# Inverting the chunk matrices of a gated delta rule: 64x64 blocks in two tiles, or 32x32 blocks in four

## The reference

```python
def step(S, inp):
    q_t, k_t, v_t, g_t, b_t = inp
    S = S * jnp.exp(g_t)[..., None, None]
    kv = jnp.einsum('bhk,bhkv->bhv', k_t, S)
    delta = (v_t - kv) * b_t[..., None]
    S = S + k_t[..., :, None] * delta[..., None, :]
    o = jnp.einsum('bhk,bhkv->bhv', q_t, S)
    return (S, o)
```

## Time and profile before

| | us |
|---|---|
| median of 3 runs | 808.12 (807.68 to 809.06) |
| the profiled execution | 807.6 |
| its span, first to last instruction | 805.9 |
| TensorE busy in the span | 662.2 (82%) |
| VectorE busy | 404.2 (50%) |
| ScalarE busy | 324.5 (40%) |

### The profile page before, as it was taken

One profiled execution on the slowest core, in us unless ns is written; L12 is line 12 of the kernel. 1 busy time (PEld: TensorE's weight loads), 2 busy tenths in 40 slices (PEclk: granted clock), 3 DMA queues, 4 the chain that ended last, 5 costly groups with the idle time before them and its releaser, 6 DMA issues. The chain is left out here.

```text
span 805.9 us, 19964 instructions
## 1 busy us (share of the span) xinstructions
PE 662.2 (82%) x8150; PEld 506.7 (63%) x8150; DVE 404.2 (50%) x911; ACT 324.5 (40%) x881; POOL 136.9 (17%) x211
## 2 busy tenths in 40 slices
PE   5789989898999999957875999989895652479995
PEld 3456666655666666635664466689895541479885
DVE  6437788854355555145773557457646463011111
ACT  1245555525444444425773541521243230233331
POOL 2012110120000000033333420650000213111121
PEclk9779999999999999958887889999998775699999
DMA  6930000036000000040000000000000038881110
GB/s 173 352 102 2 3 2 2 16 122 142 1 2 1 2 1 2 1 133 2 2 2 2 0 2 2 1 2 0 2 1 1 0 102 296 315 297 51 43 48 23
DMA packets 33165, 45.36 MB, mean 56 GB/s; under 512 B 7998, under 2 KB 26175, under 8 KB 32960
## 3 DMA queue, kind: packets, MB, share of 16 engines
q1 hardware_dynamic: 28672, 33.31, 12.7%
q0 software_dynamic: 2256, 7.37, 2.8%
q10 hardware_dynamic: 2160, 3.60, 1.5%
HBM read 36.91 MB, written 7.89 MB: 56 GB/s over the span
## 5 line engine op out<-in xcount | busy, mean ns | idle before, releaser
L387 ACT ACTIVATE a_pr<-a_bank,a_nms 128x160 f32<-128x160 f32 x128 | 49.1, 391 | 41.4 <-DVE a_nms L723 38.2
L2118 ACT ACTIVATE f_hb<-f_bank,cols 128x128 f32<-128x128 f32 x96 | 34.9, 367 | 63.2 <-PE f_bank L2236 58.5
L2236 PE MATMUL f_bank<-f_xts,f_w 128*128 x384 | 51.1, 291 | 0.8 <-DVE f_xts L2188 0.8
L2236 PEld LDWEIGHTS f_bank<-f_xts,f_w 128*128 128x128 f32 x384 | 49.9, 207 | 1.7 <-issue 1.2
L2246 PE MATMUL f_bank<-f_w,f_hb 128*128 128x256 f32 x192 | 43.7, 381 | 0.0
L627 DVE TENSOR_REDUCE a_negmx<-a_bank 128x2 f32<-128x320 f32 x64 | 30.5, 476 | 23.0 <-PE a_bank L859 23.0
L2246 PEld LDWEIGHTS f_bank<-f_w,f_hb 128*128 128x128 f32 x192 | 35.9, 192 | 4.4
L2197 DVE TENSOR_TENSOR f_yb<-f_bank,rows 128x256 f32<-128x256 f32 x12 | 5.1, 425 | 58.1 <-PE f_bank L2246 58.1
L358 POOL TENSOR_TENSOR a_spr<-a_linv,a_hm 128x128 f32<-128x128 f32 x32 | 12.1, 398 | 124.3 <-DVE a_linv L676 111.5
L624 DVE COPY a_pt<-a_bank 128x512 f32<-128x512 f32 (+1 forms) x48 | 28.6, 595 | 8.3 <-PE a_bank L868 5.7
L1843 PE MATMUL e_ps<-e_ht,e_wqkv 128*128 128x512 f32 x64 | 31.5, 646 | 1.4 <-DVE e_cv L1728 1.4
(11 more groups left out here) (368 smaller groups left out, 1575.8 us busy)
## 6 DMA issues: line engine op xcount, KB each, us to landing
f_w<-in_f_w SPq DMA_DIRECT2D x16, 1024.0 KB, 10.0
slots<-a_zero POOLq DMA_DIRECT2D x1, 4112.0 KB, 18.1
f_xs<-slots ACTq DMA_DIRECT2D x13, 257.0 KB, 2.7
a_ct<-in_ctxt SPq DMA_DIRECT2D x15, 160.0 KB, 6.1
rows<-in_rows SPq DMA_DIRECT2D x1, 2120.0 KB, 9.4
x<-in_x SPq DMA_DIRECT2D x2, 512.0 KB, 5.0
b_wq<-in_b_wq SPq DMA_DIRECT2D x1, 1024.0 KB, 7.8
b_wk<-in_b_wk SPq DMA_DIRECT2D x1, 1024.0 KB, 9.8
```

What stands on the lines that cost most here:

```text
L387: i = act.activation(pr[:, p, j, k, :], s_bank[j][:, k * KW:(k + 1) * KW], ACT.Exp, bias=nms[:, p, j, k:k + 1], accum_out=rsum[:, p, 2 * j ...
L2118: act.activation(hb[:, m, :], bank[m % 4][:, 0:P], ACT.Gelu, bias=c.col("f_b1", e * FC + m)).then_inc(z["act"], 1)
L2236: j = pe.matmul(bank[m % 4][:, 0:P], w1[:, e, kk, m * P:(m + 1) * P], xts[:, bass.ds(i % 2, 1), kk, :].rearrange("p b n -> p (b n)"), star ...
```

## The change

The inverse is built on the 32x32 diagonal blocks of each system, and the 64x64 level apart:

- `x_`, `xT`, `y` and `lm` are now 32 columns a block, with four 32x32 blocks below one another in the partitions: both halves of both systems. ScalarE copies the diagonal blocks of `lT` into a tile `lc` (`diagonal`, eight copies of 32x512, four behind silu(5) and four behind silu(6)).
- Level 0 has no product: `xT` is the identity (a sixth row of the mask table) minus the mask's result, and `x_` is its transpose by VectorE's 32x32 block transposes.
- Levels 1 to 4 have y products and `xT` by `y` only; `xT` is made from `x_` by block transposes (`turned`). TensorE's levels are a loop, VectorE's and ScalarE's are written out. A product is 32x32 by 32x32, in one of four tiles on the diagonal.
- The last level works on the one off-diagonal 32x32 block of each system: 64 y products from `lT`, 64 from `y` and `xT`. VectorE writes the negated results into `xbd`, ScalarE copies `xT` onto its diagonal (eight copies of 32x512).
- POOL's two copies of the identity are gone.

```diff
+            def diagonal(r):
+                act.wait_ge(z["lT"], r + 1)
+                for q in range(4):
+                    rows, cols = slice(32 * q, 32 * q + 32), slice(32 * (q % 2), 32 * (q % 2) + 32)
+                    a = act.activation(lc[rows, 16 * r:16 * r + 16, :], lT[rows, 16 * r:16 * r + 16, cols], ACT.Copy)
+                a.then_inc(z["lc"], 1)
...
             act.wait_ge(z["ssq"], 1)
             inverse_lengths(0, bank[0][:, 0:32].rearrange("p (t h) -> p t h", h=HG))
-            with act.Fori(1, LEVELS) as lv:
+            for lv in range(1, LEVELS):
                 for g in range(4):
-                    act.wait_ge(z["y"], 4 * lv + g + 1)
-                    act.activation(y[:, 8 * g:8 * g + 8, :].rearrange("p a n -> p (a n)"), bank[g], ACT.Copy).then_inc(z["yout"], 1)
+                    act.wait_ge(z["y"], 4 * (lv - 1) + g + 1)
+                    act.activation(octet(y, g), bank[g][:, 0:256], ACT.Copy).then_inc(z["yout"], 1)
+            act.wait_ge(z["bdz"], 4)
+            act.wait_ge(z["xt"], 4 * (LEVELS - 1))
+            for r in range(2):
+                for q in range(4):
+                    rows = slice(32 * q, 32 * q + 32)
+                    act.activation(xbd[r][rows, :, rows], xT[rows, 16 * r:16 * r + 16, :], ACT.Copy).then_inc(z["xbd"], 1)
...
+            for g in range(4):
+                dve.transpose(octet(x_, g), octet(xT, g)).then_inc(z["x"], 1)
+            for lv in range(1, LEVELS - 1):
+                if lv < LEVELS - 2:
+                    dve.wait_ge(z["y"], 4 * lv)
+                    mask_level(lv + 1)
                 for g in range(4):
-                    dve.wait_ge(z["zx"], 8 * lv + 2 * g - 7)
-                    dve.tensor_tensor(octet(x_, g), octet(x_, g), bank[4 + g], ALU.subtract).then_inc(z["xt"], 1)
-                    dve.wait_ge(z["zx"], 8 * lv + 2 * g - 6)
-                    dve.tensor_tensor(octet(xT, g), octet(xT, g), bank[g], ALU.subtract).then_inc(z["xt"], 1)
...
+                    dve.wait_ge(z["zx"], 4 * (lv - 1) + g + 1)
+                    dve.tensor_tensor(octet(x_, g), octet(x_, g), bank[4 + g][:, 0:256], ALU.subtract).then_inc(z["x"], 1)
+                    if g:
+                        turned(g - 1, 4 * lv + g)
+                turned(3, 4 * lv + 4)
+            dve.wait_ge(z["bdz"], 4)
+            for r in range(2):
+                dve.wait_ge(z["zx"], 4 * (LEVELS - 2) + 2 * r + 2)
                 for b2 in range(2):
...
             def product(dst, lhs, rhs, g):
 
                 for a in range(8 * g, 8 * g + 8):
-                    for b2 in range(2):
-                        r = slice(64 * b2, 64 * b2 + 64)
-                        i = pe.matmul(dst[r, (a % 8) * S:(a % 8 + 1) * S], lhs[r, a, :], rhs[r, a, :], start=True,
-                                      stop=True, tile_position=(64 * b2, 64 * b2))
+                    for q in range(4):
+                        rows = slice(32 * q, 32 * q + 32)
+                        i = pe.matmul(dst[rows, (a % 8) * 32:(a % 8 + 1) * 32], lhs[rows, a, :], rhs[rows, a, :], start=True,
+                                      stop=True, tile_position=(32 * q, 32 * q))
                 return i
...
+            with pe.Fori(1, LEVELS - 1) as lv:
                 pe.wait_ge(z["lm"], lv + 1)
                 for g in range(4):
-                    pe.wait_ge(z["xt"], 8 * lv - 6 + 2 * g)
+                    pe.wait_ge(z["x"], 4 * lv + g - 3)
                     pe.nop(nofuse=True)
                     product(bank[g], lm, x_, g).then_inc(z["y"], 1)
                 for g in range(4):
                     pe.wait_ge(z["yout"], 4 * lv + g - 3)
+                    pe.wait_ge(z["xt"], 4 * lv + g - 3)
                     pe.nop(nofuse=True)
-                    if not last:
-                        product(bank[4 + g], xT, y, g).then_inc(z["zx"], 1)
-                    product(bank[g], y, xT, g).then_inc(z["zx"], 1)
...
+            pe.wait_ge(z["xbd"], 12)
```

More of the change, by code:

```diff
@@ L1678, in _ @@
             silu(5)
+            diagonal(0)
             tap(7)
             silu(6)
+            diagonal(1)
             silu(7)
@@ L1753, in _, with turned @@
             conv(7)
[L1754 to L1755 removed]
             def mask_level(lv):
[L1758 removed]
+                dve.tensor_tensor(lm[:, :, :], lc[:, :, :], mt[:, lv:lv + 1, :].to_broadcast([P, NB, 32]),
                                   ALU.mult).then_inc(z["lm"], 1)
[L1760 removed]
+            def turned(g, n):
+                dve.wait_ge(z["x"], n)
+                dve.transpose(octet(xT, g), octet(x_, g)).then_inc(z["xt"], 1)
@@ L1770, in _ @@
+            dve.wait_ge(z["xt"], 4)
             mask_level(1)
[L1771 to L1778 removed]
@@ L1947, in level @@
                     pe.wait_ge(z["yout"], 4 * lv + g - 3)
+                    pe.wait_ge(z["xt"], 4 * lv + g - 3)
                     pe.nop(nofuse=True)
-                    if not last:
-                        product(bank[4 + g], xT, y, g).then_inc(z["zx"], 1)
-                    product(bank[g], y, xT, g).then_inc(z["zx"], 1)
-            with pe.Fori(1, LEVELS - 1) as lv:
-                level(lv, False)
-            level(LEVELS - 1, True)
-            pe.wait_ge(z["xt"], 8 * (LEVELS - 1) + 4)
+                    product(bank[4 + g], xT, y, g).then_inc(z["zx"], 1)
+            for g in range(4):
+                pe.wait_ge(z["x"], 4 * (LEVELS - 2) + g + 1)
+                for a in range(8 * g, 8 * g + 8):
+                    for b2 in range(2):
+                        low, high = slice(64 * b2, 64 * b2 + 32), slice(64 * b2 + 32, 64 * b2 + 64)
+                        i = pe.matmul(bank[g][high, (a % 8) * 32:(a % 8 + 1) * 32], lT[low, a, 32:64], x_[low, a, :], start=True,
+                                      stop=True, tile_position=(64 * b2, 64 * b2 + 32))
+                i.then_inc(z["y"], 1)
+            for g in range(4):
+                pe.wait_ge(z["yout"], 4 * (LEVELS - 2) + g + 1)
+                pe.wait_ge(z["xt"], 4 * (LEVELS - 2) + g + 1)
+                for a in range(8 * g, 8 * g + 8):
+                    for b2 in range(2):
+                        low, high = slice(64 * b2, 64 * b2 + 32), slice(64 * b2 + 32, 64 * b2 + 64)
+                        i = pe.matmul(bank[4 + g][low, (a % 8) * 32:(a % 8 + 1) * 32], y[high, a, :], xT[high, a, :], start=True,
+                                      stop=True, tile_position=(64 * b2 + 32, 64 * b2))
+                i.then_inc(z["zx"], 1)
+            pe.wait_ge(z["xbd"], 12)
             for t in range(NT):
@@ L2326 @@
     s_, t_ = _np.arange(S)[:, None], _np.arange(S)[None, :]
-    levels = [(s_ // (2 * n) == t_ // (2 * n)) & (s_ // n % 2 == 0) & (t_ // n % 2 == 1) for n in (1, 2, 4, 8, 16, 32)]
+    s_, t_ = s_[:32], t_[:, :32]
+    levels = [(s_ // (2 * n) == t_ // (2 * n)) & (s_ // n % 2 == 0) & (t_ // n % 2 == 1) for n in (1, 2, 4, 8, 16)] + [s_ == t_]
     tab = _np.concatenate([_np.arange(E), _np.tile(P * _np.append(_np.arange(1, NT), N), E),
@@ L2352 @@
         "i2": i2, "i2z": i2 * (_np.arange(S) > 0).astype(_np.float32),
-        "levels": _np.tile(_np.stack(levels, 1), (2, 1, 1)).astype(_np.float32),
+        "levels": _np.tile(_np.stack(levels, 1), (4, 1, 1)).astype(_np.float32),
         "f_w1": a["L1_ffn_W1"], "f_w2": a["L1_ffn_W2"], "f_wr": a["L1_ffn_Wr"],
```

44 lines of the change are left out of this document (17 added, 27 removed).

## The result

| | before | after |
|---|---|---|
| runs compared, us | 808.59 (4 runs, 807.68 to 810.9) | 775.54 (4 runs, 772.34 to 781.77) |
| ratio, 95% interval | | 0.964 (0.9581 to 0.9699) |
| profiled execution, us | 807.6 (span 805.9) | 781.77 (span 780.0) |
| first product of the inverse | 518.74 us | 519.64 us |
| start of the block transposes of v | 584.58 us | 556.58 us |

A forecast was written before the change was run, and what follows sets the result against it. TensorE was taken to bound the inverse's levels. Gains of 8.8 (level 0), 20.3 (levels 1 to 4) and 3.6 (last level) less 0.8 (turns) made 31.9 us, from 808.1 to 776.2 us, range 769 to 787.

The forecast's parts named there:

- the signs that the prediction had named: Wrong if the level period is above 8 or below 5 us, TensorE waits for transposes, or later stages differ by over 2 us.
- Level 0 gone, gain 8.8: Level 0 moves to VectorE, hidden behind `lengths` and the logarithm; level 1 starts at 518.7 instead of 527.47: 8.8 us gained.
- The diagonal copies free: ScalarE's two groups of four 32x512 copies, 2.5 us each, fit its idle times of 2.70 and 2.67 us: cost nothing.
- Levels 1 to 4, 6.54 us each: TensorE's 512 records a level at 12.5 ns plus 0.14 us; four levels 26.2 us in place of 46.53, gain 20.3.
- the burst in L1444: Eight 64x32 tiles with 64 columns, 10.0 ns a record: the low bound for the pace of levels 1 to 4.
- VectorE's transposes at 0.35: Block transposes on VectorE cost 0.35 us each, at most 0.70, and stay hidden behind TensorE; they would decide from 1.0.
- The turn, 0.8 set aside: At each of three loop turns up to 0.53 us can surface; half of that, 0.8 us, is taken off the gain.
- The last level, 7.0: From the last z product to L1958, ended by ScalarE's eight copies: 7.0 us in place of 10.6, gain 3.6.
- The clock: Slow clock behind the wait ahead of L1958 would cost the same again behind the new wait of some 3 us: nothing counted.
- VectorE as the bound: Rival: records at 7 ns, TensorE 3.8 us a level, so VectorE's 4.2 decides; gain 42.1, 766 us; chance 0.08.
- Half clock: Rival: TensorE gets 1.2 GHz in the levels, 14.9 ns a record, levels 31.1 us; gain 24.3, 784 us; chance 0.15.
- The rival that ends slower: Rival: small products don't pay, 29.2 ns a record, levels 60.4 us; 3.3 us lost, 811 us; chance 0.04.

The follow-up runs named there:

- the second trace: The changed kernel run again with no edit: 779.31 us (6 runs), ratio 0.9641 to the kernel before.
- the run that takes the cover away: The changed kernel, but VectorE starts all of level 0 only behind ScalarE's logarithm: 786.78 us, ratio 0.9747 to the kernel before.

## Why the prediction was right, and where its sizes were off

The total (776.2 for 775.54, or 778.1 over ten runs) and the mechanism hold: TensorE was the bound of the levels, the small tiles overlap, level 0 and the transposes hide, and ScalarE ends the last level. But the total is right partly by luck. An error of nearly 6 us was met by others; and of the first comparison's 33.1 us the profiled stage shows only 28.5 (27.4 in the second trace), so that a median within 0.7 us of the forecast owes something to the spread of the runs. By two of the signs that the prediction had named, it was wrong: level 1's period is 12.38 us, above 8, and the stages behind the inverse differ by 2.1 us, above 2. The transposes of v start at 556.58 and not at about 552. From the start of `lengths` to the transposes of v before took 584.58 - 514.68 = 69.90 us and the change takes 556.58 - 515.14 = 41.44: 28.5 us gained, where the steps said 31.9.

- *Level 0 gone, gain 8.8.* Right in its mechanism, and shown by the run that takes the cover away (a 6.23 us wait). Level 1's start is 0.45 us later than forecast, since 0.87 us and not 0.42 pass behind `lengths`. The profile names the logarithm, for which TensorE waited before the change too; it was over at 519.10, 0.54 us ahead. With the loop written out the same wait is 0.43 us, so the other 0.44 are the entry of the loop, for which the forecast had no term. VectorE was done at 514.90, 1.3 later than my 513.6: it starts later by 0.4, and its second mask took 2.18 us where the first took 1.23. POOL was at work beside it from 511.08 on; whether that is the reason no run tests.
- *The diagonal copies free.* Right: two groups of 2.53 us for my 2.5, and ScalarE still stood idle 0.27 and 0.24 us ahead of the tap and the silu behind them. (The 0.50 us in a row that I took as the lower price was read from PSUM, while these copies read SBUF.)
- *Levels 1 to 4, 6.54 us each.* This is the step that was wrong in size, in both directions. Levels 2 to 4 took 16.81 us and not 19.6, since records in the later passes need 9.2 to 10.0 ns, the low end of my bounds and a little under it, not their middle: the burst in L1444 was the right neighbour, and my objection that a long series would be slower was unfounded. Level 1 took 12.38 and not 6.54: 5.8 us lost to a limit that the forecast didn't have, the first fetch of the loop's instructions (4.6 us of stops; the rest is slower records and the turn). Together 29.2 for 26.2 us.
- *VectorE's transposes at 0.35.* Right, 0.35 apart (16 with 0.42 us busy each), and hidden; the run with twice as many confirms it.
- *The turn, 0.8 set aside.* It did surface: 0.31, 0.45 and 0.42 us idle at three turns, 1.2 us in all, where the kernel before shows no idle time at a turn. It lies within the 12.38 and the 16.81 above, and so isn't counted a second time below.
- *The last level, 7.0.* It took 7.75. The y products were 1.9 us as forecast; the eight copies 0.64 each and not 0.55, which I had bounded at 0.63.
- *The clock.* I counted nothing. The stages behind 556.58 took 223.4 us, and those behind 584.58 before took 221.3: 2.1 us more in the profiled pair, with a granted clock of 0.50 from 626.4 to 677.5 us, where before has it from 653.3 to 663.4 and from 666.9 to 697.5. In the other traces of these experiments the same stages took from 218.7 to 225.3 us, so this is the spread of one execution to the next, not a cost of the change.

Over the steps: 31.9 - 0.45 - 5.84 + 2.81 + 0.8 - 0.75 = 28.5 us. The change came to `lengths` 0.5 us later and took 2.1 more behind: 25.9, and the two profiled executions differ by 807.6 - 781.8 = 25.8.

The rivals. *VectorE as the bound* needed 7 ns a record and 4.2 us for VectorE; with 9.2 to 10.0 ns and VectorE at some 3.8 it didn't come to it. *Half clock* was true of nearly all of level 1 and of the first 2 us of level 2 (5 in the second trace), and such a record took 13.4 to 13.6 ns and not 14.9. (The high end of the range, 787, is some 1.5 us above what its terms give, 784 and three turns of 0.53.) The rival that ends slower stood on 29.2 ns a record with its turning point at 27.7, and I gave it 0.04. Its time came true in the kernel with its loop written out, by another mechanism: at 27.2 ns of supply and more that kernel takes as long as the one before, 812.65 us. A small product doesn't cost what this rival made it cost; what it can cost is the supply of its instructions. The Trainium skill, TensorEngine Tiling (Array Packing), section Instruction Overhead, gave 60 cycles, an estimate of 25 ns at 2.4 GHz, as a matmul's price however few its columns. The loop's 9.2 to 10.0 ns speak against it where four tiles alternate.

## What to carry to other kernels

When a change turns few large instructions into many small ones, price the supply of instructions as well as their execution: here straight TensorE code got a load and a product every 27 to 31 ns, so products shorter than that pay only in a loop's later passes, and the first pass still pays the full rate. The loop asks little for it: 0.3 to 0.45 us at a turn, for 8 to 9 us saved in each later pass. A trace can't show such a limit while each instruction takes longer than it; look at how near the present pace (29.2 ns here) may stand to something that it hides. And a piece of work moved into another's shadow doesn't keep its duration: 32 small products took 3.63 us ahead of the inverse and 6.43 behind it.

## What the runs showed of the hardware that I had not expected

- TensorE's straight code of small products (about 10 to 14 ns a record) stops once in every 128 pairs of load and product, for 0.9 to 2.2 us, once the first 201 to 234 pairs have run. Straight code of 29.2 ns a record doesn't stop. 128 pairs are one packet of 16.4 KB on the instruction queue (0.90 MB in 55), counted in two kernels (12 packets for 1,536 pairs, 9 for 1,152). With stops of 1.5 us the period is 3.48 us, with 1.8 it is 3.75. Of it the packet itself takes about 1 us.
- A loop of 512 such pairs meets these stops in its first pass only, and its three or four later passes add no packet. Such a loop costs 0.44 us at its entry and 0.3 to 0.45 us at each turn.
- Four 32x32 tiles on the diagonal sustain 9.2 ns from record to record over 256 records at 2.4 GHz, and 13.4 to 13.6 ns at 1.2 GHz: half the clock costs less than half the pace.
- The granted clock fell to 1.2 GHz close to the start of level 1 in every trace. In the changed kernel it was low from 520.5 to 534.2 us, in its second trace from 522.3 to 539.4, that is 2 and 5 us into level 2; with the loop written out it was low for 71.7 us, stops and all. Where `lengths` didn't stand ahead of level 1, it fell only 5.1 and 4.5 us behind the level's first product, in place of 0.5 to 1.3. Before the change it was low from 520.1 to 523.5, in the products of level 0, and again from 526.9 to 530.3, around the start of level 1. Why it falls and comes back no run here tests.
